# Cross-attention and LoRA feed-forward on one core: all five queues in a new order, filler matmuls in the lead-in, one-column sums in halves

## What is computed

```python
x = x + matmul(fake_quant(layernorm(x)), fake_quant(ctx))        # per batch, 8 bit, scales given
def ffn(x):                                                      # on layernorm of the new x
    probs = softmax(x @ W_router.T); w = top-2 of probs, normalised   # 8 experts
    h = einsum('td,erd->ter', x, lora_A)                         # rank 16
    return x @ W_base.T + b_base + einsum('ter,eor,te->to', h, lora_B, w) * 2
x = x + ffn(layernorm(x))
```

## Time and profile before

| | us |
|---|---|
| median of 3 runs | 966.05 (965.92 to 966.56) |
| the profiled execution | 965.27 |
| its span, first to last instruction | 963.5 |
| TensorE busy | 926.9 (96%) |
| VectorE busy | 583.1 (61%) |
| ScalarE busy | 506.8 (53%) |
| GpSimd busy | 309.5 (32%) |

### The profile page before, as it was taken

One profiled execution on the slowest core, in us unless ns is written; L12 is line 12 of the kernel. 1 busy time (PEld: TensorE's weight loads), 2 busy tenths in 40 slices (PEclk: granted clock), 3 DMA queues, 4 the chain that ended last, 5 costly groups with the idle time before them and its releaser, 6 DMA issues.

```text
span 963.5 us, 12922 instructions
## 1 busy us (share of the span) xinstructions
PE 926.9 (96%) x4518; PEld 438.4 (45%) x4538; DVE 583.1 (61%) x730; ACT 506.8 (53%) x494; POOL 309.5 (32%) x249
## 2 busy tenths in 40 slices
PE   1899999999999999999999999999999999999998
PEld 0654444544444444454444444444444444444443
DVE  6776966989787855565878877235532524325421
ACT  4866896468875647555585665434421423342420
POOL 3266887263533152452212212050210202111200
PEclk9999999999999999999999999999999999999999
DMA  8999898879953677747679767997314323342331
GB/s 309 361 357 363 336 328 326 299 276 292 282 127 106 231 231 229 245 112 260 176 232 265 177 230 186 332 318 237 103 34 116 50 93 65 99 126 71 88 66 44
DMA packets 61444, 197.07 MB, mean 205 GB/s; under 512 B 5696, under 2 KB 22208, under 8 KB 52928
## 3 DMA queue, kind: packets, MB, share of 16 engines
q1 hardware_dynamic: 55904, 176.26, 50.9%
q0 software_dynamic: 5472, 19.93, 12.6%
HBM read 137.44 MB, written 56.62 MB: 201 GB/s over the span
## 4 chain that ended last, share of the span: by engine, by line
PE 58%; issue 6%; DVE 3%; DMA 2%; POOL 2%; ACT 1%; DVEq 0%; POOLq 0%; ACTq 0%; SPq 0%
PE PS L1451 17%; PE PS L1452 17%; PE PS L1453 17%; PE PS L1464 1%; PE PS L1466 1%; PE PS L1465 1%; DMA out_dram<-Q 1%; PE PS L1144 1%; DMA S<-in_wT_dram 1%; PE PS L1068 1%; PE PS L1069 1%; PE PS L1070 1%; POOL S L1409 1%; DVE S L790 0%; DVE XA L1013 0%
## 5 line engine op out<-in xcount | busy, mean ns | idle before, releaser
L1451 PE MATMUL PS<-XA,Q 128*128 128x512 f16 x384 | 145.6, 379 | 0.0
L1453 PE MATMUL PS<-XA,Q 128*128 128x512 f16 x384 | 145.6, 379 | 0.0
L1452 PE MATMUL PS<-XA,Q 128*128 128x512 f16 x384 | 145.6, 379 | 0.0
L1409 POOL TENSOR_TENSOR S<-S 128x1024 f16<-128x1024 f32 x29 | 64.5, 2228 | 166.8 <-ACT S L1403 166.8
L683 PE MATMUL PS<-Q,S 128*128 128x512 bf16 x502 | 112.5, 382 | 2.9 <-DVE S L698 2.2
L683 PE MATMUL PS<-EX,S 128*128 128x512 bf16 (+1 forms) x534 | 107.1, 359 | 4.0 <-DVE S L663 2.5
L1403 ACT ACTIVATE Q<-S 128x1024 f16<-128x1024 f32 x64 | 66.6, 1050 | 71.4 <-PE PS L1453 29.2
L1358 ACT ACTIVATE S<-S,WC 128x1024 f32<-128x1024 f32 x64 | 70.8, 1138 | 51.2 <-DMA S<-in_wT_dram 35.3
L1451 PE MATMUL PS<-EX,S 128*128 128x512 f16 x256 | 97.0, 379 | 0.1
L1453 PE MATMUL PS<-EX,S 128*128 128x512 f16 x256 | 97.0, 379 | 0.0
L1452 PE MATMUL PS<-EX,S 128*128 128x512 f16 x256 | 97.0, 379 | 0.0
(11 more groups left out here) (239 smaller groups left out, 1697.9 us busy)
## 6 DMA issues: line engine op xcount, KB each, us to landing
...
out_dram<-Q POOLq DMA_DIRECT2D x30, 512.0 KB, 5.6
EX<-in_xn_dram SPq DMA_DIRECT2D x24, 512.0 KB, 6.4
...
XA<-in_xT_dram SPq DMA_DIRECT2D x16, 512.0 KB, 8.3
out_dram<-XA SPq DMA_DIRECT2D x16, 512.0 KB, 7.4
out_dram<-S SPq DMA_DIRECT2D x16, 512.0 KB, 4.3
```

The costliest lines, as they stand in the source:

```text
L1409: e.tensor_tensor(v[:, 1024:2048], W_SRC[n], v[:, 0:1024], ALU.subtract).then_inc(w_lo.of(i, n), 1)
L1451: e.matmul(bank(bk), wh, yh(op, k), start=(fresh and k == 0), stop=False, skip_group_check=not fresh)
L1452: e.matmul(bank(bk), wh, yl(op, k), start=False, stop=False, skip_group_check=not fresh)
L1453: last = e.matmul(bank(bk), wl, yh(op, k), start=False, stop=(read and k == 7), skip_group_check=not fresh)
```

## The change

The code changes are these (the tables and the five lists are new throughout; of the tables three lines stand here):

```diff
-CTXQ = {'a': [0, 2, 3, 4, 5, 6, 7, 8, 9, 10, 11, 12, ...], 'd': [1]}
+CTXQ = {'a': [0, 3, 6, 7, 8, 9, 11, 13, ...], 'd': [1, 2, 4, 5, 10, 12, 15, 26, 27]}
...
+    def warm(e, n, at=None):
+        e.wait_ge(*const["mean"])
+        if at is not None:
+            e.wait_ge(*xn_in[0, at, 1])
+        v = mean_w[:, :].bitcast(BF16)[:, 0:128]
+        for _ in range(n):
+            e.matmul(bank(3)[:, 0:128], v, v, start=True, stop=True)
...
     def ctx_conv(e, g):
         if g >= 3:
-            e.wait_ge(*gemm[{3: 1, 4: 0}.get(g, g - 2), 1])
+            for h in range(2):
+                e.wait_ge(*gemm[{3: 1, 4: 0}.get(g, g - 2), h])
...
+    def offset_total(e, p):
+        e.wait_ge(*sum0[NT - 1])
+        e.wait_ge(*back[1, 6, 0])
+        for t in range(4 * p, 4 * p + 4):
+            last = e.matmul(bank(4)[:, TT + t:TT + t + 1], acc0[:, 128 * t:128 * (t + 1)], mean_w[:, 0:1], start=True, stop=True)
+        last.then_inc(off_sum.of(p), 1)
-    def var_total(e, b):
+    def var_total(e, b, p):
...
-        for src, c in ((acc, 0),) if b else ((acc, 0), (acc0, TT)):
-            for t in range(TT):
-                last = e.matmul(at[:, c + t:c + t + 1], src[:, 128 * t:128 * (t + 1)], mean_w[:, 0:1], start=True, stop=True)
-        last.then_inc(var_sum.of(b), 1)
+        for t in range(4 * p, 4 * p + 4):
+            last = e.matmul(at[:, t:t + 1], acc[:, 128 * t:128 * (t + 1)], mean_w[:, 0:1], start=True, stop=True)
+        last.then_inc(var_sum.of(b, p), 1)
...
     def sync_first(e):
-        load_par(e); xn_load(e, 0, 0); xn_load(e, 0, 1); xn_load(e, 0, 2); xn_load(e, 0, 3)
+        load_par(e); xn_load(e, 0, 0); xn_load(e, 0, 1); xn_load(e, 0, 2); ctx_load(e, 0); xn_load(e, 0, 3); ctx_load(e, 1)
     def vector_program(e):
-        ln1_stats(e, 0, 0); ln1_stats(e, 0, 1); ln1_quant(e, 0, 0); ln1_stats(e, 0, 2); ln1_stats(e, 0, 3)
+        ln1_stats(e, 0, 0); ln1_stats(e, 0, 1); ln1_stats(e, 0, 2); ln1_quant(e, 0, 1); ln1_stats(e, 0, 3); ctx_quant(e, 1)
     def pool_program(e, general):
-        ln1_coef(e, 0, 0); ln1_coef(e, 0, 1); ln1_coef(e, 0, 2); ln1_coef(e, 0, 3); ln1_coef(e, 0, 4); ctx_conv(e, 1)
+        ln1_coef(e, 0, 0); ln1_coef(e, 0, 1); ranks(e); ln1_coef(e, 0, 2); ctx_conv(e, 0); ln1_coef(e, 0, 3); ctx_conv(e, 1)
```

More of the change, by code:

```diff
@@ L303, in xattn_lora_ffn @@
     sq1_ok = signal("sq1", range(1, NT))
-    var_sum = signal("var_sum", range(NB))
+    off_sum = signal("off_sum", range(2))
+    var_sum = signal("var_sum", [(b, p) for b in range(NB) for p in range(2)])
     var_off = signal("var_off", range(2))
@@ L1754, in tensor_program @@
[L1754 to L1755 removed]
+        gemm1(e, 0, 768, 1024, 0, 16); gemm1(e, 2, 768, 1024, 0, 16); gemm1(e, 3, 0, 512, 0, 8)
+        gemm1(e, 3, 512, 1024, 0, 8); ln1_turn(e, 1, 0); gemm1(e, 3, 0, 512, 8, 16); gemm1(e, 4, 0, 512, 0, 8)
+        ln1_turn(e, 1, 1); gemm1(e, 3, 512, 1024, 8, 16); gemm1(e, 4, 512, 1024, 0, 8); gemm1(e, 4, 512, 1024, 8, 16)
@@ new lines, in vector_program @@
+        var_diag(e, 1); w_add(e, 3, 4); w_low(e, 3, 2); w_low(e, 3, 6); w_add(e, 3, 5); w_low(e, 3, 4)
+        y_scale(e, 1, 0, "A"); y_scale(e, 1, 0, "B"); y_diff3(e, 1, 0); y_diff1(e, 1, 0); y_diff2(e, 1, 0)
+        y_low(e, 1, 0, "A"); y_diff4(e, 1, 0); y_low(e, 1, 0, "T"); y_low(e, 1, 0, "4"); y_low(e, 1, 0, "B"); w_norm(e, 4)
+        w_seen(e, 4); post(e, 3, 4); w_factors(e, 4); y_scale(e, 1, 1, "A"); y_scale(e, 1, 1, "B"); y_diff3(e, 1, 1)
+        y_diff1(e, 1, 1); w_low(e, 4, 0); y_diff2(e, 1, 1); y_low(e, 1, 1, "A"); y_diff4(e, 1, 1); y_low(e, 1, 1, "B")
@@ new lines, in vector_program @@
+        y_low(e, 1, 1, "T"); w_add(e, 4, 1); post(e, 3, 5); w_low(e, 4, 1); w_add(e, 4, 2); w_low(e, 4, 3); w_low(e, 4, 2)
+        w_add(e, 4, 4); w_add(e, 4, 5); w_low(e, 4, 4); y_scale(e, 1, 2, "A"); y_scale(e, 1, 2, "B"); w_low(e, 4, 6)
+        y_diff3(e, 1, 2); y_diff1(e, 1, 2); b_low(e, 4); y_diff2(e, 1, 2); y_low(e, 1, 2, "A"); y_diff4(e, 1, 2)
+        post(e, 4, 1); w_norm(e, 5); w_seen(e, 5); w_factors(e, 5); post(e, 4, 4); w_add(e, 5, 1); y_scale(e, 1, 3, "A")
+        y_scale(e, 1, 3, "B"); y_diff3(e, 1, 3); y_diff1(e, 1, 3); y_diff2(e, 1, 3); y_low(e, 1, 3, "A"); y_diff4(e, 1, 3)
@@ new lines, in vector_program @@
+        y_low(e, 1, 3, "B"); w_low(e, 5, 1); w_add(e, 5, 2); w_add(e, 5, 4); w_low(e, 5, 2); y_low(e, 1, 3, "T")
+        post(e, 4, 5); w_add(e, 5, 5); w_low(e, 5, 4); w_low(e, 5, 5); y_scale(e, 1, 4, "A"); y_scale(e, 1, 4, "B")
+        y_diff3(e, 1, 4); y_diff1(e, 1, 4); y_diff2(e, 1, 4); b_low(e, 5); y_low(e, 1, 4, "A"); y_diff4(e, 1, 4)
+        post(e, 5, 1); w_norm(e, 6); w_seen(e, 6); post(e, 5, 4); w_factors(e, 6); w_add(e, 6, 1); b_low(e, 6)
+        y_scale(e, 1, 5, "A"); y_scale(e, 1, 5, "B"); y_diff3(e, 1, 5); y_diff1(e, 1, 5); y_diff2(e, 1, 5); w_add(e, 6, 2)
@@ new lines, in vector_program @@
+        y_low(e, 1, 5, "A"); y_diff4(e, 1, 5); y_low(e, 1, 5, "B"); y_low(e, 1, 5, "4"); w_low(e, 6, 2); y_low(e, 1, 5, "T")
+        post(e, 5, 5); w_add(e, 6, 4); w_add(e, 6, 5); w_low(e, 6, 6); w_low(e, 6, 5); y_scale(e, 1, 6, "A")
+        y_scale(e, 1, 6, "B"); y_diff3(e, 1, 6); y_diff1(e, 1, 6); y_diff2(e, 1, 6); y_diff4(e, 1, 6); post(e, 6, 1)
+        w_norm(e, 7); w_seen(e, 7); w_factors(e, 7); y_low(e, 1, 6, "4"); post(e, 6, 4); w_add(e, 7, 1)
+        y_scale(e, 1, 7, "A"); w_add(e, 7, 2); w_add(e, 7, 4); y_scale(e, 1, 7, "B"); w_low(e, 7, 6); w_low(e, 7, 4)
@@ new lines, in vector_program @@
+        y_diff3(e, 1, 7); y_diff1(e, 1, 7); post(e, 6, 5); w_low(e, 7, 2); y_diff2(e, 1, 7); w_low(e, 7, 3)
+        y_low(e, 1, 7, "A"); y_diff4(e, 1, 7); b_low(e, 7); w_add(e, 7, 5); w_low(e, 7, 5); y_low(e, 1, 7, "T")
+        y_low(e, 1, 7, "4"); y_low(e, 1, 7, "B"); a_low(e, 1, 0); a_low(e, 1, 1); post(e, 7, 1); post(e, 7, 4)
+        post(e, 7, 5); w_add(e, 8, 1); w_low(e, 8, 1); w_add(e, 8, 2); w_low(e, 8, 0); w_add(e, 8, 4); lora_sums(e, 1)
+        w_low(e, 8, 2); w_low(e, 8, 6); w_low(e, 8, 3); w_low(e, 8, 4); w_add(e, 8, 5); w_low(e, 8, 5); route_logits(e, 1)
@@ L1975, in pool_program @@
-        store(e, 13, 0); w_low(e, 14, 2); w_low(e, 15, 2); w_low(e, 15, 3); store(e, 13, 1); store(e, 14, 0)
-        store(e, 14, 1)
+        ln1_coef(e, 0, 0); ln1_coef(e, 0, 1); ranks(e); ln1_coef(e, 0, 2); ctx_conv(e, 0); ln1_coef(e, 0, 3); ctx_conv(e, 1)
+        ln1_coef(e, 0, 4); ln1_coef(e, 0, 5); ctx_conv(e, 2); ln1_coef(e, 0, 6); ln1_coef(e, 0, 7); ln1_coef(e, 1, 0)
+        ln1_coef(e, 1, 1); ctx_conv(e, 4); ln1_coef(e, 1, 2); add0(e, 1); add0(e, 2); ln1_coef(e, 1, 3); add0(e, 3)
+        ln1_coef(e, 1, 4); ctx_conv(e, 7); ln1_coef(e, 1, 5); ln1_coef(e, 1, 6); ctx_conv(e, 10); sqadd0(e, 1); sqadd0(e, 2)
@@ new lines, in pool_program @@
+        sum1_move(e, 8); ctx_conv(e, 27); x_add(e, 26, general); y_low(e, 0, 3, "T"); ctx_conv(e, 29); add1(e, 10)
+        add1(e, 11); y_low(e, 0, 4, "A"); ctx_conv(e, 31); add1(e, 12); x_add(e, 29, general); y_low(e, 0, 4, "T")
+        add1(e, 13); y_low(e, 0, 5, "A"); sum1_move(e, 14); y_low(e, 0, 5, "T"); w_root(e, 0); y_low(e, 0, 6, "A")
+        y_low(e, 0, 6, "T"); x_add(e, 31, general); add1(e, 15); w_low(e, 0, 1); y_low(e, 0, 7, "A"); y_low(e, 0, 7, "T")
+        w_low(e, 0, 3); w_low(e, 0, 2); w_low(e, 0, 6); sqsum1_move(e, 1); w_root(e, 1); w_low(e, 1, 1); sqadd1(e, 2)
@@ new lines, in pool_program @@
+        sqsum1_move(e, 3); w_low(e, 1, 4); store(e, 0, 0); w_low(e, 1, 2); w_low(e, 1, 6); sqadd1(e, 4); sqadd1(e, 6)
+        w_root(e, 2); store(e, 0, 1); sqadd1(e, 8); sqadd1(e, 9); sqadd1(e, 10); store(e, 1, 0); w_low(e, 2, 5)
+        w_root(e, 3); store(e, 1, 1); sqadd1(e, 14); sqadd1(e, 15); store(e, 2, 0); var_root(e, 1); w_low(e, 3, 5)
+        w_root(e, 4); y_low(e, 1, 1, "4"); store(e, 2, 1); store(e, 3, 0); w_low(e, 4, 5); y_low(e, 1, 2, "4")
+        y_low(e, 1, 2, "B"); y_low(e, 1, 2, "T"); w_root(e, 5); w_low(e, 5, 0); y_low(e, 1, 3, "4"); store(e, 3, 1)
@@ new lines, in pool_program @@
+        w_low(e, 5, 3); store(e, 4, 0); w_low(e, 5, 6); y_low(e, 1, 4, "B"); y_low(e, 1, 4, "4"); y_low(e, 1, 4, "T")
+        w_root(e, 6); w_low(e, 6, 1); store(e, 4, 1); w_low(e, 6, 0); w_low(e, 6, 3); store(e, 5, 0); w_low(e, 6, 4)
+        y_low(e, 1, 6, "A"); y_low(e, 1, 6, "B"); y_low(e, 1, 6, "T"); w_root(e, 7); w_low(e, 7, 0); w_low(e, 7, 1)
+        store(e, 5, 1); store(e, 6, 1); store(e, 6, 0); store(e, 7, 0); store(e, 7, 1); store(e, 8, 0); store(e, 8, 1)
+        store(e, 9, 0); store(e, 9, 1); store(e, 10, 1); store(e, 10, 0); store(e, 11, 0); store(e, 11, 1); store(e, 12, 0)
@@ L1978, in xattn_lora_ffn @@
+        store(e, 12, 1); store(e, 13, 1); store(e, 13, 0); store(e, 14, 0); store(e, 14, 1)
     with nc.Block() as block:
```

643 lines of the change are left out of this document (299 added, 344 removed), and 88 rows, old and new, of tables (EVAC, GEMM, POST, PROD).

## The result

The changed kernel takes 991.59 us (median of 4 runs, 985.81 to 994.43) against 966.3 (965.92 to 967.55) before: a ratio of 1.0256, 95% interval 1.023 to 1.0281. It is slower by 25 us. Its four runs lie 8.6 us apart; the four of before lie 1.6 apart here, and its 11 to 20 runs beside each group of experiments lie 6 to 10 apart. The profiled execution took 991.01 us, its span is 989.2.

A forecast was written before the change was run, and what follows sets the result against it. TensorE was taken as the bound, never waiting from 372 us on, with gains only earlier. From 965.27, -7.7 - 1.9 - 1.0 + 1.1 gave 955.8 for the profiled execution, 956.5 from the median; range 951 to 964.

The forecast's parts named there:

- Lead-in, -7.7: Start to about 58 us: first product at about 21.3 us for 28.91, saving 7.7 us, bounds -10 and -4.
- One-column sums, -1.9: Batch 0's sixteen sums near 170 us: no longer in one row, the clock stays high; -1.9 us, between 0 and -1.9.
- Later waits, -1.0 with -4 to +6: TensorE's waits up to 292 us and at 371.8, with work moved between engines: -1.0 us, bounds -4 and +6.
- Rival B: Lead-in gain given back by 300 us as waits for DVE's chain to the last y_low: 962 to 964.5 us; chance 0.07.
- rival C: Batch 1's two stage buffers: denser traffic lengthens store and load landings, each round pays; slower, 971 us; chance 0.06.
- w_low from pair 8 on, nothing: 21 w_low moved to DVE from pair 8 on, where DVE has much idle time: no effect.
- DVE shutting POOL out: DVE's roundings block POOL: at most 6.5 us added to POOL's work before 292 us, where it is idle; sum unchanged.
- End, +1.1: After the last matmul: two posts wait and two stores are issued behind the second, costing 1.1 us.
- Signs: Trace marks listed to show the forecast right or wrong, such as first product at 20 to 23 us, or later than 24.

The follow-up runs named there:

- e2: Old order of all queues up to about 300 us, the changed kernel's new order behind it: 987.55 us, 1.02 of before.
- e12: Kernel of before with only the new lead-in, plus batch 0's first eight one-column sums moved ahead in two groups of four: 956.85 us, 0.9908 of before.
- e3: The changed kernel with all queues in the order of before from pair 9 on (about 700 us): 988.71 us, 1.021 of before.
- e6: The changed kernel with 54 second-stage w_low and y_low back on their old engine (DVE or POOL): 993.83 us, 1.0294 of before.
- e9: The changed kernel with pair 8's first two w_scale on ACT moved behind batch 1's last y_high and w_high(7, 5): 984.76 us, 1.0203 of before.
- e10: The changed kernel with weight norms of pairs 1 and 3 summed later on TensorE and some posts moved ahead on DVE: 994.79 us, 1.0293 of before.
- e7: New first stage and old second-stage order, with the new DVE/POOL division of 54 w_low and y_low: 974.8 us, 1.0093 of before.
- e4: The changed kernel without its 76 filler matmuls: 984.68 us, 1.02 of before.

## Why the prediction was wrong

It said 956.5 us, 951 to 964; it was 991.6.

**The step that failed** is the reading of the earlier trace rows from 372 us on: "in that part no order can gain, it can only lose", and then no term for the loss. The sum priced the moves up to 300 us, 21 `w_low` and the end; the other steps of a new order of five queues over 660 us stood at zero, without bounds, and no rival had its place there. It is where the kernel lost most of its 25 us: 21 in e2, where only this part is new; in the ledger +15.8 of waits and the larger part of the clock's, at `w_total`, at posts, at the loads of y. A TensorE that never waits had been read as one that is safe; it says nothing of how much time the steps it depends on have in hand. That the other engines had room there (DVE 304 and ACT 258 of 588 us) made it look safe too.

Point by point:
- **Lead-in, -7.7.** The chain was right: the first product at 20.29 for 21.3 forecast, the products of 512 columns at 48.8, inside 48.5 to 50.5, and one low spell in it. The term was if anything too careful (9.8 us at that point). Kept to the end with the old order behind: 5.9 of 8.9 us in the profile.
- **One-column sums, -1.9.** Right: windows of 10 us at 165 and at 170 print a clock of 1.00 in the changed kernel, and taking the row apart removed the spell in e12. One of its grounds was weak: a spell of 3.4 us among batch 1's eight would take 0.3% off the mean of 588 us, which still prints as 1.00. A window of 5 us at 420 does print 1.00 in before, so the ground holds.
- **Later waits, -1.0 with -4 to +6.** The wrong side: up to 292 us +7.6 of idle, outside the bound. Rival B (0.07) came true in the first stage: at the start of the second the two kernels are level, 273.78 for 273.31. Its mechanism was half right. The costliest wait of the first stage, 3.80 at 235.0, is for an x that landed 10 us after its issue at 224.13, behind a load of context at 221.46, which is rival C's place more than B's.
- **w_low from pair 8 on, nothing.** Not contradicted from pair 9 on (e3, 2.9 us less, not clear of noise).
- **DVE shutting POOL out.** Weighed as harmless before 292 us. No run takes DVE's new roundings back alone; e6 changes the division only behind them, and was no faster. So nothing here shows it as the cause, and nothing prices it.
- **End, +1.1.** +1.5: the last two posts and three stores in a row,

```profile
984.45 1.41 DVE L1526 SCALAR_TENSOR_TENSOR Q<-PS,WC,Q 128x512 f32<-128x512 f32 x2 [9.53 <-PE PS L1485]
985.23 1.49 SPq L510 DMA_DIRECT2D out_dram<-Q  x3
```

- **Signs.** The text listed idle time of at most 4 us "between there and 300" and nothing behind 300. The signs had the same hole as the sum. The turn of batch 1's first tile, expected at 49 to 52, came at 52.06, the end of the span 4.8 us behind the last matmul for 4.4.

A term for the second stage would have been a number of failing hand-offs times a price for each. The profile of before gave one such price, 2.14 us with no fall of the clock; the runs show 1 to 5 us of waiting plus 0 to 3.4 of clock, at eight places behind 300 us. I would not have known how many fail, but slower would have had far more than 0.06.

What stays open: why the new order is worse at its places, beyond the steps held behind a late load or norm that e9 and e10 show; the new division's own price (e7); and the 0.5% of e4.
